# GATv2 loops: the transpose of the split logits placed ahead of the sum of a group instead of behind it

## What is computed

```python
xl = x @ Wl
xr = x @ Wr
ee = eattr @ We
xj = xl[src]
h = jax.nn.leaky_relu(xj + xr[dst] + ee, SLOPE)
logits = h @ att
m = jax.ops.segment_max(logits, dst, n)
ex = jnp.exp(logits - m[dst])
denom = jax.ops.segment_sum(ex, dst, n)
alpha = ex / denom[dst]
out = jax.ops.segment_sum(xj * alpha[:, None], dst, n)
```

## Time and profile before

| | |
|---|---|
| median of 3 runs | 6522.72 us (6521.69 to 6536.36) |
| the profiled execution | 6535.35 us, of it the span 6533.6 us |
| TensorE, matmuls | 4991.3 us busy, 76% |
| TensorE, weight loads | 3639.1 us, 56% |
| VectorE | 4608.6 us, 71% |
| ScalarE | 3312.4 us, 51% |
| GpSimd | 3155.9 us, 48% |

### The profile page before, as it was taken

One profiled execution on the slowest core, in us unless ns is written; L12 is line 12 of the kernel. 1 busy time (PEld: TensorE's weight loads), 2 busy tenths in 40 slices (PEclk: granted clock), 3 DMA queues, 4 the chain that ended last, 5 costly groups with the idle time before them and its releaser, 6 DMA issues. The chain is left out here.

```text
span 6533.6 us, 112163 instructions
## 1 busy us (share of the span) xinstructions
PE 4991.3 (76%) x28188; PEld 3639.1 (56%) x28558; DVE 4608.6 (71%) x17132; ACT 3312.4 (51%) x8567; POOL 3155.9 (48%) x3442
## 2 busy tenths in 40 slices
PE   5999877985778777886687877777366766666799
PEld 2444444863656555664465655556255555555578
DVE  8999876254777777776577767777577777777721
ACT  5888765023555555553455545555355555555520
POOL 2444333634556555650565656554255555555400
PEclk9999988997999999998899999999689999999899
DMA  2233334853444444441444444443234443443264
GB/s 57 62 89 100 94 100 143 318 191 95 106 107 109 108 107 106 107 100 36 102 108 108 108 102 108 105 106 80 59 92 103 102 103 101 104 102 103 74 160 114
DMA packets 606739, 698.65 MB, mean 107 GB/s; under 512 B 243043, under 2 KB 512656, under 8 KB 599802
## 3 DMA queue, kind: packets, MB, share of 16 engines
q0 software_dynamic: 128832, 362.75, 22.0%
q1 hardware_dynamic: 477370, 329.75, 18.4%
HBM read 589.91 MB, written 102.19 MB: 106 GB/s over the span
## 5 line engine op out<-in xcount | busy, mean ns | idle before, releaser
L980 POOL DMA_INDIRECT gath<-table,src_col x880 | 846.7, 962 | 873.5 <-issue 601.8
L980 POOL DMA_INDIRECT h<-table,src_col x880 | 841.3, 956 | 574.9 <-issue 574.9
L1119 PE MATMUL psum<-xr 128*128 x3520 | 1031.8, 395 | 35.5 <-ACT xr L1081 18.0
L703 DVE SCALAR_TENSOR_TENSOR xr<-xr,gath,psum 128x259 f32<-128x259 f32 x1440 | 685.8, 476 | 108.0 <-PE psum L687 82.2
L1068 ACT CAST rows<-psum 128x128 bf16<-128x128 f32 x440 | 116.7, 265 | 1134.0 <-remote 684.8
L1204 POOL DMA_INDIRECT gath<-table,src_col x440 | 423.6, 963 | 490.3 <-issue 327.3
L1119 PEld LDWEIGHTS psum<-xr 128*128 128x128 f32 x3520 | 545.8, 196 | 200.5 <-issue 50.2
L999 DVE SCALAR_TENSOR_TENSOR zs<-zs,mean 128x256 f32<-128x256 f32 x1760 | 649.3, 423 | 0.0
L1005 DVE TENSOR_REDUCE seen<-psum 128x1 f32<-128x512 f32 x440 | 303.4, 690 | 470.5 <-PE psum L1130 321.4
L1204 POOL DMA_INDIRECT h<-table,src_col x440 | 422.0, 959 | 297.8 <-issue 297.8
L687 PE MATMUL psum<-zs,locrow 128*128 128x259 f32 x1440 | 468.1, 452 | 117.0 <-POOL zs L642 94.3
(11 more groups left out here) (330 smaller groups left out, 11988.3 us busy)
## 6 DMA issues: line engine op xcount, KB each, us to landing
locrow<-g_locb SPq DMA_DIRECT2D x660, 128.0 KB
pairs<-xr SPq DMA_DIRECT2D x640, 115.5 KB
xr<-pairs SPq DMA_DIRECT2D x13, 1716.0 KB
gath<-table,src_col POOLq DMA_INDIRECT x1320
h<-table,src_col POOLq DMA_INDIRECT x1320
xr<-pairs SPq DMA_DIRECT2D x25, 832.0 KB
acc<-pairs SPq DMA_DIRECT2D x12, 1716.0 KB
xr<-pairs SPq DMA_DIRECT2D x13, 1584.0 KB
```

The costliest lines, as they stand in the source:

```text
L703: nc.vector.scalar_tensor_tensor(kept[:, u, 0:EXTRA + 3], kept[:, (u - 1) % HELD, 0:EXTRA + 3], t["same"][:, g:g + 1], m.ps[u % 4][:, 0:EX ...
L980: pool.indirect_dma_start(m.gath[r][:, j, :], None, table, bass.IndirectOffsetOnAxis(m.src_col[r][:, j:j + 1], 0)).then_inc(gathered[r], 16)
L1119: nc.tensor.matmul(zb[q][:, j, :], m.hot[r][:, j, :], blk(m.xr, b, 0, D), start=True, stop=False)
```

## The change

In the list of stages of TensorE in `gatv2_loop`, `turn_parts` goes from the first place with lag 3 to the place ahead of `sum_group` with lag 2. Group t's parts are thus transposed in slot t + 2, between `mix` of group t + 1 and `sum_group` of group t - 2, where before it was the first of slot t + 3, behind that same `sum_group`. Nothing else is touched.

```diff
-            straight([(3, turn_parts), (4, flip), (3, show_logits), (1, mix), (4, sum_group)],
+            straight([(4, flip), (3, show_logits), (1, mix), (2, turn_parts), (4, sum_group)],
                       blocks_on(nc, m, mybir.EngineType.PE))
```

## The result

The changed kernel takes **6655.36 us** (median of 4 runs, 6644.90 to 6663.70) against 6522.2 us before (4 runs, 6504.22 to 6536.36): ratio 1.0205, 95% interval 1.0181 to 1.0230. It is 2.0% slower, and outside the range of 6410 to 6600 us. The profiled execution took 6644.90 us, its span 6643.2, at a mean granted clock of 0.922 where it was 0.941.

What follows compares the result with a forecast made beforehand. A circle through GpSimd's gathers and TensorE's late completions was taken to bound the loops. Wait terms counted 0, sums seen early -31 us: 6535.35 to 6504 us, less 12.6 for the median: 6492 us, range 6410 to 6600.

Steps and rivals of the forecast that it cites:

- The circle through GpSimd: GATv2 loop body: three gather steps, 2.05 us until TensorE's completions get through, 0.7 to the next gather: 6.5 us a group.
- The wait taken away: TensorE before show_logits: copied rows are ready, up to 0.99 us a group less idle time, worth 0 in a locked slot.
- The wait added: TensorE before the moved transpose: waits 0.6 us for VectorE's split; sum_group still ends 0.8 us earlier.
- What is left: How often GpSimd sees sum_group early in the loop bodies: between +31 and -62 us, taken as -31 us.
- a pair of 12.64 us: Two groups in the loop body when sum_group is seen before the gathers are over: 6.32 us each.
- "worst" end: Both loops with all slots locked: 6.53 instead of 6.46 us a group, +31 us over 440 groups.
- a locked one: Loop body slot where sum_group's completion is seen only 2.0 us after the fourth gather starts: 6.53 us.
- Rival 2: When a sum is seen early, eight gathers run joined: 15.6 us a pair instead of 12.9; 6612 us, chance 0.24.
- Rival 1: TensorE's wait for rows bounds the loops, completions don't depend on gathers: -436 us, 6087 us; chance 0.09.
- What would show it: Trace signs: rows wait under 0.3 us, transpose wait 0.5 to 1.3, pace 6.3 to 6.55, loop's end near 5.0.

Runs made afterwards that it cites:

- nog_after: Changed kernel with GpSimd gathering only the first ten groups of each GATv2 loop: 5923.31 us, against 5897.18 for the old order with the same edit.
- the paced kernels: Old and changed order, each group's gathers also waiting until three of the group before have landed: 6389.94 and 6389.76 us, both 0.9799 of the kernel before.
- waitparts_before: Kernel before, with sum_group also waiting for the split of group t + 2; chip without the hold: 5601.03 us, 1.0152 of the kernel before.
- again_waitparts: Kernel before, with sum_group also waiting for the split of group t + 2; chip with the hold: 6576.95 us, 1.0061 of the kernel before.
- pace4_after: Changed kernel, with each group's gathers also waiting until all four of the group before have landed: 7334.87 us, one run.

## Why the prediction was wrong

- *The circle through GpSimd* was right on chips with the hold: 5.05 us a group without gathers, 6.4 to 6.5 with them. It isn't the 2.0 us "after the start of the last gather" in every slot, though. Of the 195 copies in the body of `before`, 101 start 1.4 us or more after the modelled end of their transpose and 50 less than 0.15 us after it. In the changed kernel a copy started at 2311.47, 0.6 us after its transpose, with gathers around it. Such early completions are what a train needs to join; what decides which completion gets through early stays open.
- *"The wait taken away ... worth 0"*: right in kind. 163 us of idle time left the place (193.4 to 30.1) and nothing was gained.
- *"The wait added"* was priced at 0.6 us a group and at no cost. It is 1.13 us a group in the trace of the changed kernel, and alone it costs 37 us, 0.08 us a group. This term was missing from the sum. `nog_after` (+26 us, one run each) shows that a part of it has nothing to do with gathers: it arises where the block numbers are read, which I had said "stays in either order". At the loop's end the forecast of 0 held: 4.96 us a group, for 4.99.
- **The step that failed is "What is left".** I counted every sum seen early as a pair of 12.64 us, gaining 0.14 us a group, and took two thirds of the way to the better end, -31 us. "More completions should slip through" was right as far as the joined trains tell. But what slipped through joined trains (116 instead of 31), and the gain per pair never came: from the 21st split to the 211th the two loops run at 6.86 and 6.77 us a group, where the kernel before has 6.46 and 6.55. That is beyond the "worst" end of 6.53, which assumed that no slot could be longer than a locked one. The two ends were not bounds, and instead of -31 us the change cost 133.
- *Rival 2* names the mechanism. Its price for a pair was near (15.6 us for 15.8 measured with all trains forced); its number was not. I gave the joins to the turns where block numbers are read, 44; there were 85 more than before. From 90 us over 85 trains each costs about 1.1 us net, less than the 2.7 worked out, perhaps since such a train also starts earlier. That the rival's upper end, +119, lies near the +117 of the two loops is luck: more trains than assumed, at a lower price, and the 37 us of the wait besides.
- *The clock* was priced nowhere. It is the part that stays open. In the profiled execution slow sums take 111 us more than before (125 less 14), nearly all of the loss if each were on the circle. With all trains forced it is 0.7 of 2.9 us a pair in the old order, but some 130 of the 188 us by which the new order is slower there. In the changed kernel the long pauses all go with joined trains; shorter ones and slow sums also come without (40 slow sums in the paced kernels). How many of the 90 us pass through the clock no run separates.
- *Rival 1* and the rule behind it (the Trainium skill, SBUF, Who interferes with whom: DMA and compute don't contend) don't hold on the chips with the hold: 6.46 us a group with gathers, 5.05 without. The rule speaks of SBUF's ports; what holds the completions back here no run shows. On the two other chips the trace agrees with the rule. The changed kernel itself wasn't run there; with the added wait it was slower there as well (+1.5% and +2.0%).
- *What would show it*: the wait for rows fell under 0.3 us (0.16), the wait before the transpose came out in 0.5 to 1.3, VectorE's wait for show_logits grew (0.96 to 1.33 us) where it should have shrunk a little, and the pace didn't stay in 6.3 to 6.55. Of the two signs named for rival 2, trains of eight are plain (103 for 11). Slots over 9 us are there from one `sum_inputs` to the next (119, before 41), but hardly from split to split (27, before 23).

## What to carry to other kernels

An engine that is locked to another's train of transfers may gain nothing from work made ready earlier, and can lose by it: running ahead changes when the train is released, and here two trains became one, at a higher price than two. Bound such a term by a slot that is longer than any seen, not by the worst slot of the trace before. And before tuning to a stall, ask whether it belongs to the kernel or to the chip on which it was profiled.

## What the runs showed of the hardware

- The same kernel takes 5515 us on some chips (two of the six on which runs of this study fell) and 6522 to 6544 on others, 18% apart. One kernel was profiled on both kinds: `waitparts_before` and `again_waitparts` have the same program, with spans of 5606 and 6571 us. Each GATv2 loop takes 1147 us from first to last split on the one and 1474 and 1467 on the other, the third loop 1154 and 1472 from first to last gather. These three differences, 326, 320 and 318 us, make up all of the 964: in this pair the two kinds of chip differ only in the loops in which GpSimd gathers. TensorE's completion reaches ScalarE 0.04 us after the modelled end in every slot on the one kind; on the other, in `before`, it takes 1.4 us or more in half of the slots. What makes a chip one or the other stays open.
- Where a gather's release isn't held back, it starts 0.78 us after the modelled end of the sum that it waits for (2322.83 to 2323.61). It lands some 3.5 us after its own start, by the estimate from `pace4_after`.
- After pauses of 3.78 and 3.79 us TensorE ran at a granted clock of 0.50 and 0.61: 1.97 us of sum_group became 3.77 and 3.14.
